# A graph kernel: the last chunk's source rows fetched one by one on SyncE instead of gathered on GpSimd

## The reference

```python
# first network, L = 4 layers, 8 heads of 16
q = (h @ Wq.T + bq)[dst];  k = (h @ Wk.T + bk)[src];  v = (h @ Wv.T + bv)[src]
alpha = sum(q * k, -1) / 4
ex = exp(alpha - segment_max(alpha, dst)[dst])
a = ex / segment_sum(ex, dst)[dst]
out = segment_sum(a * v, dst)           # then gate, layer norm, feed-forward
# second network, once
msg = silu(concat(x[src], x[dst], rbf(len)) @ mw1 + mb1) @ mw2 + mb2
agg = segment_sum(msg, dst) / count     # then update and layer norm
```

## Time and profile before

| | us |
|---|---|
| median of three runs | 7938.27 |
| lowest and highest run | 7920.73, 7941.61 |
| the profiled execution | 7866.28 |
| its span, first to last instruction | 7864.5 |
| TensorE, VectorE, ScalarE, GpSimd busy | 4591.8, 4054.1, 2762.9, 3848.5 |

### The profile page before, as it was taken

How to read it: one execution, slowest core, us unless ns; L and a number is a source line. 1 busy time by engine, 2 the same in 40 slices (tenths; PEclk the granted TensorE clock), 3 DMA queues, 4 the chain that set the end, 5 groups by cost and what they waited for, 6 DMA issues and landing times.

```text
span 7864.5 us, 105863 instructions
## 1 busy us (share of the span) xinstructions
PE 4591.8 (58%) x22799; PEld 3687.8 (47%) x22800; DVE 4054.1 (52%) x11127; ACT 2762.9 (35%) x6393; POOL 3848.5 (49%) x4061
## 2 busy tenths in 40 slices
PE   4555555655555556555555565555555655666666
PEld 2444444534444445344444453444444544555555
DVE  4555555645555556455555564555555653333334
ACT  1333333423333334233333342333333432333333
POOL 3555555335555553345555543455555425555553
PEclk6666666676666666766666667666666677878788
DMA  4222222122222222222222222222222211111111
GB/s 127 78 78 74 78 78 77 52 66 76 78 77 79 76 79 57 65 69 77 77 79 77 79 61 68 68 78 78 78 76 80 60 31 44 44 45 45 45 44 27
DMA packets 267185, 536.12 MB, mean 68 GB/s; under 512 B 116251, under 2 KB 148687, under 8 KB 266507
## 3 DMA queue, kind: packets, MB, share of 16 engines
q0 software_dynamic: 180992, 490.24, 23.2%
q1 hardware_dynamic: 78899, 35.89, 1.8%
q10 hardware_dynamic: 6936, 6.69, 0.3%
HBM read 512.41 MB, written 18.03 MB: 67 GB/s over the span
## 4 chain that ended last, share of the span: by engine, by line
PE 27%; another core or an unknown queue 25%; issue 20%; DVE 17%; ACT 5%; DVEq 4%; ACTq 1%; DMA 0%; SPq 0%; POOL 0%; POOLq 0%
PE bank L765 9%; PE bank L784 8%; DVE acc L1191 6%; PE bank L769 2%; PE bank L756 2%; ACT oh L549 2%; DVEq L330 2%; PE bank L805 2%; PE bank L833 1%; DVE alpha L1214 1%; DVEq L1191 1%; DVE slots L1283 1%; DVE oh L1175 1%; PE bank L937 1%
## 5 line engine op out<-in xcount | busy, mean ns | idle before, releaser
L504 POOL DMA_INDIRECT slots<-kv_table,idx x3224 | 3065.0, 951 | 3149.1 <-PE bank L784 1272.7
L784 PE MATMUL bank<-slots,oh 128*128 128x136 f32 (+1 forms) x8060 | 1598.6, 352 | 584.7 <-DVE acc L1191 502.7
L765 PE MATMUL bank<-qs,ohT 128*128 x8080 | 1676.3, 354 | 230.3 <-ACT ohT L540 132.0
L784 PEld LDWEIGHTS bank<-slots,oh 128*128 128x128 f32 x8060 | 1415.4, 253 | 716.9 <-DVE acc L1191 614.8
L765 PEld LDWEIGHTS bank<-qs,ohT 128*128 128x128 f32 x8080 | 1428.7, 256 | 450.4 <-issue 428.3
L1191 DVE TENSOR_TENSOR acc<-acc,bank 128x136 f32 (+1 forms) x4030 | 1173.6, 291 | 603.7 <-PE bank L784 166.4
L1208 DVE TENSOR_TENSOR slots<-slots,bank 128x512 f32<-128x512 f32 x808 | 552.3, 684 | 1312.1 <-remote 1294.4
L540 ACT ACTIVATE ohT<-bank,miss 128x512 f32<-128x512 f32 x1010 | 676.5, 683 | 1360.0 <-PE bank L756 1226.6
L504 POOL DMA_INDIRECT slots<-src_table,idx x806 | 760.8, 944 | 750.5 <-DMA idx<-src_e 233.6
L549 ACT ACTIVATE oh<-iota,rel_e 128x128 f32<-128x128 f32 x3168 | 962.9, 387 | 0.0
L797 PE MATMUL bank<-ident,alpha 128*128 128x128 f32 x204 | 93.7, 459 | 1459.5 <-DVE alpha L1214 1423.0
(11 more groups left out here) (255 smaller groups left out, 4032.7 us busy)
## 6 DMA issues: line engine op xcount, KB each, us to landing
slots<-kv_table,idx POOLq DMA_INDIRECT x3224
kv_table<-slots SPq DMA_DIRECT2D x20, 660.0 KB, 3.4
slots<-src_table,idx POOLq DMA_INDIRECT x806
resets<-flat_len ACTq DMA_DIRECT2D x51, 128.0 KB
idx<-src_e SPq DMA_DIRECT2D x255, 8.0 KB
terms<-flat_rel SPq DMA_DIRECT2D x255, 12.0 KB
resets<-flat_rst SPq DMA_DIRECT2D x2, 1551.0 KB
w<-in_w SPq DMA_DIRECT2D x8, 256.0 KB
```

Of the source, the lines that this page charges most:

```text
L504: pool.indirect_dma_start(slots[:, k, t, 0:width], None, table, bass.IndirectOffsetOnAxis(ap=idx[:, k, t:t + 1], axis=0))\
L765: mm = pe.matmul(o, ohT[:, j % 2, t, :], qs[:, blocks[j * G + t], 0:HID], start=True, stop=basis is None)
L784: mm = pe.matmul(bank[6 + part % 2][:, o:o + width], oh[:, k % 2, t, :], slots[:, k, t, HID:HID + width], start=True, stop=True)
```

## The change

A table `far_table` in DRAM has one row for each of the 768 edges of the last chunk's six places. During a pass SyncE copies their rows from the node table into it, DRAM to DRAM, one transfer a row. The node numbers were put once, at the start, into one partition of SBUF (`far_src`, in free partitions of the tile of `terms`); SyncE loads 16 of them at a time into registers (`fetch_rows`). In the loop it does so behind the staging of each chunk, 44 times 16 rows; behind the loop twice 32. Then it waits for all rows (two semaphores, for even and odd rows) and for the two groups of the ring to come free, and one transfer brings the six places into `slots`. VectorE waits for that one (`far_in`) in the last chunk. GpSimd gathers 800 places a pass; its counters of uses go on as before.

```diff
--- before.py
+++ after.py
@@ -54,6 +54,11 @@
 ROUNDS = 4
 LAST_PLACES = PLACES - (CHUNKS - 1) * CH
 LAST_NG = -(-LAST_PLACES // G)
+FAR_FIRST = (CHUNKS - 1) * CH
+FAR_ROWS = LAST_PLACES * P
+FAR_STEP = 16
+FAR_LOOPED = (FULL - 1) * RING * FAR_STEP
+FAR_ENDS = [FAR_LOOPED + (FAR_ROWS - FAR_LOOPED) * (k + 1) // 2 for k in range(2)]
 START = (RING - 1) * NG + 1
 NBASIS = 16
 STACK = P // NBASIS
@@ -89,6 +94,8 @@
 
         kv_table = nc.dram_tensor("kv_table", [NPAD, KVW], F32, kind="Internal").ap()
         src_table = nc.dram_tensor("src_table", [NPAD, HID], F32, kind="Internal").ap()
+        far_flat = nc.dram_tensor("far_flat", [FAR_ROWS], I32, kind="Internal").ap()
+        far_table = nc.dram_tensor("far_table", [FAR_ROWS, KVW], F32, kind="Internal").ap()
         flat_dst = nc.dram_tensor("flat_dst", [VC * P * P + P], F32, kind="Internal").ap()
         flat_rst = nc.dram_tensor("flat_rst", [2, CH, VC * HEADS, RW], BF16, kind="Internal").ap()
         flat_len = nc.dram_tensor("flat_len", [VC * P * P], F32, kind="Internal").ap()
@@ -105,7 +112,9 @@
         centers = sb("centers", [P, 1])
         miss = sb("miss", [P, 1])
         spread = sb("spread", [3 * NG, NG, P], BF16)
-        terms = sb("terms", [3 * NG, RING, G * P], BF16)
+        terms_tile = sb("terms_tile", [P, RING, G * P], BF16)
+        terms = terms_tile[0:3 * NG, :, :]
+        far_src = terms_tile[64:65, :, :].rearrange("p a b -> p (a b)").bitcast(I32)[:, 0:FAR_ROWS]
         ones = sb("ones", [P, NB])
 
         h = sb("h", [P, NB, HID])
@@ -262,6 +271,7 @@
         act_req, act_ans = sem("act_req"), sem("act_ans")
         node_done, acc_zero = sem("node_done"), sem("acc_zero")
         idx_in = sems("idx_in", RING)
+        far_named, far_even, far_odd, far_in = [sem(f"far_{n}") for n in ("named", "even", "odd", "in")]
         kv_in = [sems(f"kv_in{k}_", NG) for k in range(RING)]
         slot_free = [sems(f"slot_free{k}_", NG) for k in range(RING)]
         oh_far = sem("oh_far")
@@ -312,10 +322,12 @@
 
         def landed(l, i, k, j):
 
-            lost = min(max((j + 1) * G - LAST_PLACES, 0), G) if k == REM - 1 else 0
-            short = lost if isinstance(i, int) and i == FULL else 0
-            a_pass = G * (FULL + (k < REM)) - lost
-            return 16 * a_pass * l + (16 * G * (i + 1) - 16 * short if isinstance(i, int) else 16 * G * i + 16 * G)
+            a_pass = G * (FULL + (k < REM - 1))
+            return 16 * a_pass * l + (16 * G * (i + 1) if isinstance(i, int) else 16 * G * i + 16 * G)
+
+        def is_last(i, k):
+
+            return isinstance(i, int) and i == FULL and k == REM - 1
 
         def bc(ap, n):
 
@@ -393,12 +405,33 @@
                 for k in range(RING):
                     load_indices(k, k)
 
-            def stage_layer(l):
+            def fetch_rows(first, count, table, width):
+
+                for at in range(0, count, FAR_STEP):
+                    _, rows = nc.values_load_multi_w_load_instructions(
+                        far_src[0:1, bass.ds(first + at, FAR_STEP)], [mybir.EngineType.SP], min_val=0, max_val=N - 1,
+                        skip_runtime_bounds_check_because="an edge's source is the number of a node, and padding holds 0")
+                    for n, row in enumerate(rows):
+                        sp.dma_start(far_table[bass.ds(first + at + n, 1), 0:width], table[bass.ds(row, 1), 0:width])\
+                            .then_inc((far_even, far_odd)[n % 2], 16)
+
+            def stage_layer(l, table, width):
                 with sp.Fori(1, FULL) as i:
                     for k in range(RING):
+                        sp.wait_ge(tab_out, 16 * NI * (l + 1))
                         stage_indices(k, l, i)
+                        fetch_rows((RING * i + (k - RING)) * FAR_STEP, FAR_STEP, table, width)
                 for k in range(REM):
                     stage_indices(k, l, FULL)
+                    if k < len(FAR_ENDS):
+                        first = FAR_ENDS[k - 1] if k else FAR_LOOPED
+                        fetch_rows(first, FAR_ENDS[k] - first, table, width)
+                sp.wait_ge(far_even, 8 * FAR_ROWS * (l + 1))
+                sp.wait_ge(far_odd, 8 * FAR_ROWS * (l + 1))
+                for j in range(LAST_NG):
+                    sp.wait_ge(slot_free[REM - 1][j], START + (FULL + 1) * l + FULL)
+                sp.dma_start(slots[:, REM - 1, 0:LAST_PLACES, 0:width],
+                             far_table[:, 0:width].rearrange("(t p) k -> p t k", p=P)).then_inc(far_in, 16)
 
             load_keys(0)
             load_queries(0)
@@ -407,6 +440,8 @@
             store_table(0)
             sp.wait_ge(su_rows, 16 * VC)
             sp.dma_start(flat_len.rearrange("(c p e) -> p c e", p=P, e=P), rows_l.bitcast(F32)).then_inc(su_len, 16)
+            sp.dma_start(far_flat.rearrange("(t e) -> t e", e=P),
+                         rows_i[FAR_FIRST % P:FAR_FIRST % P + LAST_PLACES, FAR_FIRST // P, :]).then_inc(far_named, 16)
             sp.wait_ge(su_taken, VC)
             for k in range(RING):
                 load_sources(k, k)
@@ -435,8 +470,11 @@
                                  flat_rst[i][:, first:end, :].rearrange("t c e -> t (c e)").unsqueeze(0)
                                  .to_broadcast([HEADS, CH, (end - first) * RW])).then_inc(landed_all, 16)
             sp.wait_ge(su_far, 32)
+            sp.wait_ge(far_named, 16)
+            sp.dma_start(far_src[0:1, :], far_flat.unsqueeze(0)).then_inc(far_named, 16)
+            sp.wait_ge(far_named, 32)
             with sp.Fori(0, L - 1) as l:
-                stage_layer(l)
+                stage_layer(l, kv_table, KVW)
                 stage_first(l + 1)
                 sp.wait_ge(a_ev, START + NB * (l + 1))
                 load_keys(l + 1)
@@ -444,7 +482,7 @@
                 load_queries(l + 1)
                 store_table(l + 1)
                 load_layer(l + 1)
-            stage_layer(L - 1)
+            stage_layer(L - 1, kv_table, KVW)
             stage_first(L)
             sp.wait_ge(h_new, START + 2 * NI * L)
             sp.dma_start(m_1c, a["m_1c"].rearrange("p (q k) -> p q k", q=STACK)).then_inc(ld_basis, 16)
@@ -454,11 +492,7 @@
                 sp.wait_ge(dst_ps, START + i + 1)
                 sp.dma_start(src_table[i * GW:(i + 1) * GW, :].rearrange("(b p) k -> p b k", p=P),
                              kvst[:, i * BW:(i + 1) * BW, 0:HID]).then_inc(tab_out, 16)
-            with sp.Fori(1, FULL) as i:
-                for k in range(RING):
-                    stage_indices(k, L, i)
-            for k in range(REM):
-                stage_indices(k, L, FULL)
+            stage_layer(L, src_table, HID)
             for i in range(NI - 1):
                 sp.wait_ge(out_ready, START + i + 1)
                 sp.dma_start(out[i * GW:(i + 1) * GW, :].rearrange("(b p) k -> p b k", p=P), out_rows[i]).then_inc(out_sent, 16)
@@ -506,8 +540,10 @@
                             .then_inc(kv_in[k][j], 16)
 
             def gather_rest(l, table, width):
-                for k in range(REM):
-                    gather_chunk(k, turn_of(l, FULL, k), l, table, width, min(CH, PLACES - (RING * FULL + k) * CH))
+                for k in range(REM - 1):
+                    gather_chunk(k, turn_of(l, FULL, k), l, table, width)
+                for j in range(LAST_NG):
+                    pool.reg_add(uses[REM - 1][j], uses[REM - 1][j], 1)
 
             with pool.Fori(0, L) as l:
                 with pool.Fori(0, FULL) as i:
@@ -1202,7 +1238,10 @@
             def multiply(g, l, i, k, j):
 
                 groups = groups_of(i, k)
-                dve.wait_ge(kv_in[k][j], landed(l, i, k, j))
+                if is_last(i, k):
+                    dve.wait_ge(far_in, 16 * (l + 1))
+                else:
+                    dve.wait_ge(kv_in[k][j], landed(l, i, k, j))
                 dve.wait_ge(q_spread, START + NG * g + j + 1)
                 keys = slots[:, k, j * G:(j + 1) * G, 0:HID]
                 dve.tensor_tensor(keys, keys, bank[2 + j % 2][:, :].rearrange("p (t k) -> p t k", t=G),
@@ -1326,7 +1365,10 @@
             def messages(g, i, k, j):
 
                 groups = groups_of(i, k)
-                dve.wait_ge(kv_in[k][j], landed(L, i, k, j))
+                if is_last(i, k):
+                    dve.wait_ge(far_in, 16 * (L + 1))
+                else:
+                    dve.wait_ge(kv_in[k][j], landed(L, i, k, j))
                 dve.wait_ge(q_spread, START + NG * g + j + 1)
                 dve.tensor_tensor(slots[:, k, j * G:(j + 1) * G, HID:2 * HID], slots[:, k, j * G:(j + 1) * G, 0:HID],
                                   bank[2 + j % 2][:, :].rearrange("p (t k) -> p t k", t=G), ALU.add)\
```

## The result

The changed kernel takes 9035.68 us (median of 4 runs, 9021.33 to 9040.74), beside 7939.94 us for the kernel before (4 runs): ratio 1.1387, interval [1.1368, 1.1406]. The forecast was 7918 us. It was wrong, and by far: the change costs 1096 us, where a gain of 20 was expected.

The account below looks back on a forecast made before the run. The prediction took late TensorE signals during back-to-back gathers, with no engine full, to bound the kernel. It summed -20.5 us removed, +0.6 at the start and 0 disturbance to -19.9 us: 7918 us, range 7888 to 7985.

Parts of the forecast that it names:

- What bounds the kernel: Steady step: no engine full; TensorE's signals reach others late during back-to-back gathers, with one VectorE wait of 7.36 us.
- Removed, -20.5 us from four waits: Last six gathers of each pass go, ending VectorE's waits of 5.24, 5.37, 5.39 and 4.51 us: -20.5 us.
- Added on SyncE: Loop step: 16 rows at 0.8 us, a register load and two existing transfers, 15.5 of 27 us, costing nothing.
- Do the new transfers disturb anything?: Whole run: small DRAM writes beside unbroken gathers had slowed nothing in the earlier trace, so disturbance was taken as 0.
- the 1.52 us that the prediction itself named as the bound: Loop step: SyncE falls behind only if a row needs more than 1.52 us, twice the 0.76 seen.
- End of pass: Two steps of 32 rows take SyncE 29.4 us against 27.9, making it 1.5 us late to the next stage.
- 40 us of cover: End of pass: slack before VectorE needs the 811 KB transfer; gone if SyncE were 1.5 us a row slower over 64 rows.
- Rival 4: Loop: a row exceeds 1.52 us as a queue fills; at 2 us, 34.7 us a step, 1694 us more; chance 0.04.
- Rivals 1 to 3: Larger gain, 24 to 38 us (0.20); nothing goes, 7938 us (0.10); SyncE's work slows each step, 7989 us (0.16).
- Rival 3: SyncE's new work lengthens each step, clearest at VectorE's register load, up to 0.31 us: +51 us, 7989 us; chance 0.16.

Follow-up runs that it names:

- e10: Changed kernel with SyncE's job varied by layer (rows, fixed-address transfers, nothing) and pauses after every four gathers in half the message pass: 5963.05 us beside 5662.62.
- e14: The same kernel as e10, run again where the kernel before is at the slower level: 8270.03 us beside 7868.89.
- e17: The same kernel as e1, run again where the kernel before takes about 7925 us: ratio 0.9990.
- e1: Changed kernel without row transfers and register loads, the last transfer reading the table as it lies: 5667.10 us beside 5659.75, ratio 1.0012.
- e5: The changed kernel itself, run again where the kernel before is at the quicker level: 5721.29 us beside 5657.84, ratio 1.0115.

## Why the prediction was wrong

By its own steps:

- *What bounds the kernel: signals of TensorE are late while gathers run back to back.* Right at this level, and more general than I took it. At the other level VectorE has no "remote" wait, though gathers run back to back in hundreds; with pauses the two levels agree (e10, e14).
- *Removed, -20.5 us from four waits.* Where SyncE does nothing new (e17) the waits went, 15.4 us of 20.5 in one trace, and the kernel gained 0.1% [0, 0.2], not 0.25%. At the level of 5660 us nothing was gained (e1). So even without the rows the forecast's own change would have been hard to measure.
- *Added on SyncE: 0.8 us a row, 13.9 + 1.6 = 15.5 us of a step, cost 0.* **This step failed**, twice. First, the row alone is 1.055 us: four instructions and their gaps, of which I had 0.6 + 0.2, the 0.2 without a row that shows it. With the measured 3.8 us for the rest a step is 20.6 us, still under 27. That would have cost nothing here; at the other level it costs 1.15% (e5).
- *"Do the new transfers disturb anything? So I take 0."* The question was put the wrong way round. What mattered was what the gathers do to SyncE. I had read that TensorE's signals come 7 us late beside gathers, and I treated it as a property of those signals; SyncE's new work was priced from rows free of it, L429 in the earlier trace rows, single instructions without address arithmetic. Gathers ran without a break beside those too, and nothing was late; why not there stays open, and one such window was too little to carry a zero for 230 steps. The trace of the kernel before had the sign all along: L356, SyncE's own register instruction at that wait, has a median of 0.129 us and a longest of 1.000, and eleven such instructions of SyncE and VectorE took over 0.6 us, each during a run of gathers or within 3 us of one. This is the second failure, and the one that made the loss: four instructions at 1.4 us are 5.6 us a row, over the 1.52 us that the prediction itself named as the bound. The block of 14 us a step turns 20.6 into 34.9.
- *End of pass, 29.4 against 27.9 us, 40 us of cover.* Wrong in size: the blocks of 32 rows take 45.78 and 45.93 us here. The transfer of 811 KB landed in 4.6 us, just under the 5 to 10 of the estimate. The cover was thought larger than it was: SyncE 1.5 us slower on each of 64 rows is 96 us, while 12 us up to the freed groups and 40 behind them were there, so it ends at 0.8 us a row. It held all the same, since the steps had become longer too; no wait of VectorE on this transfer stands in the trace.
- *Rival 4*, a row over 1.52 us, at 2 us a row 34.7 us a step. That is what happened: 2.0 us, 34.9 us. It got 0.04. Its cause was put as "a queue fills up"; e14's fixed transfers, as many and as large, speak against that. So the size of this rival was met by another mechanism. Its price of 1694 us took 7.7 us for each of 220 steps; measured are 274 us a layer (6.2 us for 44 steps, since the steps of a layer's start are shorter) and 68 in the message pass, whose shorter rows leave a step of 28.4 us.
- *Rivals 1 to 3* did not decide anything. Rival 3 had the right engine, SyncE's new work in each step, but VectorE's register load, its clearest place, was not what grew.

Not settled: what sets the level (5660 or 7900 us), what exactly delays the other engines' instructions there, and how long a step would be with the register instructions of the rows and none of their transfers, since the kernels meant for that held none. Nor was it tried whether scattered rows cost more than the 16 fixed ones of e14, or whether a long run of gathers and a late SyncE really feed each other.

## What to carry to other kernels

Count the instructions of an added transfer, not the transfers: a row with an address out of a register was four instructions, and it is those that the disturbed queue slowed. A wait that no signal explains may be a property of the stretch and not of the signal, as here, so look at the longest and not only the median instruction of every engine in that stretch, and price new work there by it. And when a row of an idle engine is to carry a cost of zero, ask for the step at which it stops being idle, and how far the worst row in the trace takes you towards it.
